# Chunks of 64 on quarters of the array, and other PSUM banks, in a linear-attention and mixture-of-experts layer

## The reference

```python
# attention: 8 heads of 32, q, k, v = layernorm(x) @ W.T
for chunk of 64 rows:
    inter  = q @ state                      # state: 32 x 32 per head
    scores = (q @ k.T) * tril
    intra  = scores @ v
    state  = state + k.T @ v
o     = inter + intra
denom = max(|sum(q * cumsum(k))|, 1)        # per row and head
o     = rmsnorm(o / denom, norm_w) @ Wo.T
x     = x + layernorm(o)
# experts: 8, all computed for every row, weighted by a router
h     = silu(y @ Wg[e]) * (y @ Wu[e])       # y = layernorm(x); 256 -> 256
out   = sum_e route[e] * (h @ Wd[e])
x     = x + layernorm(out)
```

## Time and profile before

| | us |
|---|---|
| three runs, median (lowest to highest) | 1700.5 (1697.83 to 1701.41) |
| the profiled execution | 1699.92 |
| its span, first to last instruction | 1698.2 |
| PE busy | 1621.4 (95%) |
| DVE busy | 1042.9 (61%) |
| ACT busy | 743.0 (44%) |
| POOL busy | 453.2 (27%) |

### The profile page before, as it was taken

How to read it: one execution, slowest core, us unless ns; L and a number is a source line. 1 busy time by engine, 2 the same in 40 slices (tenths; PEclk the granted TensorE clock), 3 DMA queues, 4 the chain that set the end, 5 groups by cost and what they waited for, 6 DMA issues and landing times. The chain is left out here.

```text
span 1698.2 us, 30395 instructions
## 1 busy us (share of the span) xinstructions
PE 1621.4 (95%) x10432; PEld 1424.6 (84%) x10432; DVE 1042.9 (61%) x2518; ACT 743.0 (44%) x1552; POOL 453.2 (27%) x750
## 2 busy tenths in 40 slices
PE   5599999999999999999999999999999999999987
PEld 4578888888888888888888888888888888888876
DVE  3555756657565665756666565666756666565655
ACT  5443544434344444444444344343534444354422
POOL 1321412324132231402323131232412223141230
PEclk9599999999999999999999999999999999999989
DMA  3200000000000000000000000000000000000000
GB/s 118 81 1 1 13 12 12 12 0 25 0 12 12 12 12 0 19 6 12 12 5 20 0 12 12 12 12 0 25 0 12 12 12 12 0 12 14 1 13 13
DMA packets 25339, 24.49 MB, mean 14 GB/s; under 512 B 2016, under 2 KB 25056, under 8 KB 25312
## 3 DMA queue, kind: packets, MB, share of 16 engines
q1 hardware_dynamic: 25312, 24.13, 4.5%
HBM read 15.74 MB, written 8.39 MB: 14 GB/s over the span
## 5 line engine op out<-in xcount | busy, mean ns | idle before, releaser
L843 DVE TENSOR_TENSOR late<-late,up_ps 128x512 f32<-128x512 f32 x256 | 174.8, 683 | 320.9 <-ACT late L648 319.1
L648 ACT ACTIVATE late<-gate_ps 128x512 f32<-128x512 f32 x256 | 152.1, 594 | 472.0 <-PE up_ps L387 448.1
L1040 POOL TENSOR_TENSOR rms_f<-rms_in,minus_half 128x8 f32<-128x8 f32 x64 | 112.1, 1752 | 698.0 <-DVE rms_in L805 698.0
L387 PE MATMUL down_ps<-w_hi,h_hi 128*128 128x256 f32 x1024 | 277.3, 293 | 8.4 <-DVE late L856 7.0
L387 PE MATMUL down_ps<-w_hi,h_lo 128*128 128x256 f32 x1024 | 263.2, 280 | 0.0
L761 DVE TENSOR_TENSOR h_lo<-late,h_hi 128x512 fp32r<-128x512 f32 x256 | 175.9, 687 | 116.2 <-ACT h_hi L566 114.0
L387 PE MATMUL gate_ps<-ft_hi,w_hi 128*128 128x512 f32 x512 | 211.7, 413 | 0.8 <-ACT ft_hi L566 0.8
L566 ACT ACTIVATE h_hi<-late 128x512 fp32r<-128x512 f32 x256 | 160.6, 627 | 117.8 <-DVE late L843 117.8
L387 PEld LDWEIGHTS down_ps<-w_hi,h_hi 128*128 128x128 f32 x1024 | 192.9, 188 | 16.6 <-DVE h_lo L761 9.0
L387 PE MATMUL gate_ps<-ft_hi,w_lo 128*128 128x512 f32 x512 | 203.7, 398 | 0.0
L387 PE MATMUL down_ps<-w_lo,h_hi 128*128 128x256 f32 x1024 | 203.6, 280 | 0.0
(11 more groups left out here) (144 smaller groups left out, 2956.1 us busy)
## 6 DMA issues: line engine op xcount, KB each, us to landing
xs<-in_x SPq DMA_DIRECT2D x32, 256.0 KB, 2.8
out_rows<-late SPq DMA_DIRECT2D x32, 256.0 KB, 2.2
late<-in_wg SPq DMA_DIRECT2D x8, 256.0 KB, 3.0
late<-in_wu SPq DMA_DIRECT2D x8, 256.0 KB, 2.7
late<-in_wd SPq DMA_DIRECT2D x8, 256.0 KB, 2.8
late<-in_wkv_t SPq DMA_DIRECT2D x1, 512.0 KB, 5.1
late<-in_wq_t SPq DMA_DIRECT2D x1, 256.0 KB, 3.3
late<-in_wo_t SPq DMA_DIRECT2D x1, 256.0 KB, 5.5
```

The source lines that it names most:

```text
L387: last = nc.tensor.matmul(dst, lhs, rhs, start=n == 0, stop=n == len(terms + low_terms) - 1)
L648: nc.scalar.activation(h_f[:, m, :], gate_ps[m][:, :], ACT.Silu).then_inc(silu_ready[0], 1)
L843: nc.vector.tensor_tensor(h_f[:, m, :], h_f[:, m, :], up_ps[m][:, :], ALU.mult).then_inc(h_ready[0], 1)
L1040: nc.gpsimd.tensor_tensor(rms_f[:, t % 2, :], rms_in[:, :], minus_half[:, :], ALU.pow)\
```

## The change

1. **Chunks of 64.** Each tile of 128 rows is two chunks, i = 0 and 1. The scores are 64 x 64 blocks, made in quarters of the array: 64 rows of contraction (r) and 64 weight columns (i), 16 matmuls a tile of 64 moving columns where there were 8 of 128. su becomes 8 matmuls of 64 x 64 weights with 66 moving columns where there were 2 of 128 x 128 with 132, and o becomes 4 state products of 128 x 64 weights and 132 moving columns and 16 products of prob and v in quarters, where there were 2 and 8.
2. **State.** DVE's su step makes two masked sums (528 values) and adds twice, since each chunk has a state of its own. o(t) now waits for su(t), so su stands ahead of o in `STEPS`, which is reordered throughout its first 19 places, as is the first block's list.
3. **kz.** Two copies with a per-partition factor (`odd_even`) instead of four copies of 32 partitions.
4. **PSUM.** One bank for gate, one for down, two for up, and four for attention as two pairs, where each step uses the first 256 columns of both banks of its pair. q and kv, of 512 columns, become two products of 256 columns each.
5. **Waits.** PE waits for silu of the gate before ahead of each gate, and for the reading of the down before ahead of each down. silu waits for gate alone (`gate_done`), hidden for up. add_down(0, 0) moves ahead of hidden(1, 1) on DVE. The last expert's written-out order goes; it is as every other.
6. **o_n, fin and prob** share an SBUF tensor, and DVE's places 1 to 3 in `first_expert` are now called.

```diff
 STEPS = [
     [("xt", 0), ("xt", 1)],
     [("kv", 0), ("q", 0)],
-    [("q", 1)],
-    [("kt", 0), ("kv", 1)],
-    [("s", 0, 0), ("s", 0, 1)],
-    [("kt", 1)],
-    [("o", 0), ("su", 0)],
-    [("s", 1, 0), ("s", 1, 1)],
-    [("kv", 2), ("keep_x1",), ("norm_stats", 0)],
-    [("kt", 2), ("o", 1), ("su", 1), ("norm_apply", 0)],
-    [("s", 2, 0), ("s", 2, 1)],
-    [("ot", 0), ("norm_stats", 1), ("kv", 3)],
-    [("kt", 3), ("o", 2), ("su", 2), ("norm_apply", 1)],
-    [("s", 3, 0), ("s", 3, 1)],
+    [("kv", 1), ("q", 1)],
+    [("kt", 0), ("su", 0)],
+    [("s", 0), ("kt", 1)],
+    [("su", 1)],
+    [("o", 0), ("s", 1)],
+    [("kv", 2), ("keep_x1",)],
+    [("kv", 3), ("norm_stats", 0)],
+    [("o", 1), ("kt", 2)],
+    [("su", 2), ("norm_apply", 0)],
+    [("s", 2), ("kt", 3), ("norm_stats", 1)],
+    [("ot", 0), ("su", 3)],
+    [("o", 2), ("s", 3), ("norm_apply", 1)],
     [("ot", 1), ("norm_stats", 2)],
-    [("o", 3), ("su", 3), ("norm_apply", 2), ("norm_stats", 3)],
-    [("wo", 0), ("ot", 2), ("norm_apply", 3)],
-    [("ln2_stats", 0)],
-    [("ln2_apply", 0), ("ot", 3)],
+    [("o", 3), ("norm_apply", 2)],
+    [("wo", 0), ("ot", 2), ("norm_stats", 3)],
+    [("norm_apply", 3), ("ln2_stats", 0)],
+    [("ot", 3), ("ln2_apply", 0)],
     [("ln2_add", 0), ("ln3_stats", 0)],
     [("wo", 1), ("ln3_apply", 0), ("ln2_stats", 1)],
...
-        gate_ps = [bank(f"gate_ps{m}") for m in range(MT)]
+        gate_ps = bank("gate_ps")
         up_ps = [bank(f"up_ps{m}") for m in range(MT)]
-        down_ps = [bank(f"down_ps{p}") for p in range(2)]
-        att_ps = [bank(f"att_ps{n}") for n in range(2)]
+        down_ps = bank("down_ps")
+        att_ps = ctx.enter_context(nc.psum_tensor("att_ps", [P, 4, 512], f32))
...
                 elif kind == "s":
-                    t, half = step[1:]
-                    if half == 0:
-                        return
+                    t = step[1]
                     reach(pe, q_ready, a, HG)
                     reach(pe, kz_ready, a, t + 1)
+                    pe.sem_inc(quarters_begun, 1)
+                    for n in range(2 * HG):
+                        g, j = divmod(n, 2)
+                        for i in range(2):
+                            for r in range(2):
+                                half = slice(64 * r, 64 * r + 64)
+                                tok = t * P + C * i
+                                last = nc.tensor.matmul(dst[C * i:C * i + C, r, C * n:C * n + C],
+                                                        kz[half, g, j, C * i:C * i + C], q_t[half, g, tok:tok + C],
+                                                        start=True, stop=True)
+                elif kind == "o":
+                    t = step[1]
+                    reach(pe, prob_ready, a, t + 1)
+                    reach(pe, v_ready, a, t + 1)
+                    reach(pe, state_ready, a, t + 1)
+                    for i in range(2):
+                        for g in range(HG):
+                            tok = t * P + C * i
+                            nc.tensor.matmul(dst[C * g:C * g + C, i, 0:HPG * VA], q_t[:, g, tok:tok + C],
+                                             state[:, t % B, t // B * 2 + i, :, g * PAIR:g * PAIR + PAIR],
+                                             start=True, stop=False)
+                    for j in range(HPG):
+                        for g in range(HG):
+                            for i in range(2):
+                                chunk = slice(C * i, C * i + C)
+                                last = nc.tensor.matmul(dst[C * g:C * g + C, i, j * VA:j * VA + VA],
+                                                        prob[chunk, j // 2, 2 * g + j % 2, :], v_sb[chunk, t, g * HPG + j, :],
+                                                        start=False, stop=j == HPG - 1)
+                elif kind == "su":
+                    t = step[1]
+                    reach(pe, v_ready, a, t + 1)
+                    pe.sem_inc(quarters_begun, 1)
...
             def up(e, m, f):
...
+                reach(pe, ft_hi_ready, f, 2)
+                reach(pe, silu_ready, f, 2 * e + m)
+                into(gate_ps, 0).then_inc(gate_done[0], 1)
+                reach(pe, h_ready, f, 2 * e + m - 1)
+                into(up_ps[m], 1).then_inc(up_done[0], 1)
 
             def down(e, p, f):
                 reach(pe, h_lo_ready, f, 2 * e + 2)
-                reach(pe, down_read, f, 2 * e + p - 1)
+                reach(pe, down_read, f, 2 * e + p)
...
             def rest(a, f):
 
-                for e in range(2, E - 1):
+                for e in range(2, E):
                     for m in range(MT):
                         up(e, m, f)
                         attention(4 * e - 4 + 2 * m, a)
                         down(e - 1, m, f)
                         attention(4 * e - 3 + 2 * m, a)
-
-                up(E - 1, 0, f)
-                up(E - 1, 1, f)
-                down(E - 2, 0, f)
-                for n in range(4 * E - 8, 4 * E - 4):
-                    attention(n, a)
-                down(E - 2, 1, f)
...
                 elif kind == "kt":
-                    for j in range(HPG):
-                        r = slice(j * D, j * D + D)
-                        last = copy(kz[r, :, j % 2, :], src[r, 0:HG * P].rearrange("p (g s) -> p g s", g=HG))
+                    for j in range(2):
+                        last = nc.scalar.activation(kz[:, :, j, :], src[:, :, 0:P], ACT.Copy, scale=odd_even[:, j:j + 1])
...
                 elif kind == "su":
                     t = step[1]
+                    b, n = t % B, t // B * 2
                     reach(dve, att_done, a, number_of(step, a) + 1)
...
+                    shape = [P, 2, 2, HG * PAIR]
+                    nc.vector.tensor_tensor(state_add[:, :, :, :],
+                                            att_half(step, a)[:, :, 0:HG * PAIR].unsqueeze(2).broadcast_to(shape),
+                                            pair_diag[:, :, :, :].broadcast_to(shape), ALU.mult).then_inc(su_read[0], 1)
                     reach(dve, su_read, a, t + 1)
...
+                    settle(nc.vector.tensor_tensor(state[:, b, n + 1, :, :], state[:, b, n, :, :], state_add[:, 0, :, :],
+                                                   ALU.add))
+                    nc.vector.tensor_tensor(state[:, b, (n + 2) % 4, :, :], state[:, b, n + 1, :, :], state_add[:, 1, :, :],
+                                            ALU.add).then_inc(state_ready[0], 1)
...
                 route_rank(f)
                 route_weights(f)
+                add_down(0, 0, f)
+                if a is not None:
+                    attention(1, a)
                 hidden(1, 1, f)
+                if a is not None:
+                    attention(2, a)
                 low_hidden(1, 1, f)
-                add_down(0, 0, f)
                 add_down(0, 1, f)
+                if a is not None:
+                    attention(3, a)
```

More of the change, by code:

```diff
@@ L31 @@
 VA = D + 1
-GV = HPG * VA
+C = 64
+PAIR = 2 * VA
 LN_EPS = 1e-5
@@ L291, in build_program @@
             READ_OUT["kt", t] = (kz_ready, t + 1)
-            for g in range(HG):
-                READ_OUT["s", t, g] = (prob_ready, HG * t + g + 1)
+            READ_OUT["s", t] = (prob_ready, t + 1)
             READ_OUT["o", t] = (o_copied, t + 1)
@@ L408, in att_step @@
                     reach(pe, xt_ready, a, KT)
-                    last = products(dst[:, :], [((wq_hi[:, k, g * P:g * P + P], wq_lo[:, k, g * P:g * P + P]),
-                                                 (xt_hi[:, k, :], xt_lo[:, k, :])) for k in range(KT)])
+                    for n in range(2):
+                        c = slice(256 * n, 256 * n + 256)
+                        last = products(dst[:, n, :], [((wq_hi[:, k, g * P:g * P + P], wq_lo[:, k, g * P:g * P + P]),
+                                                        (xt_hi[:, k, c], xt_lo[:, k, c])) for k in range(KT)])
                 elif kind == "kv":
@@ L413, in att_step @@
                     reach(pe, xt_ready, a, KT)
-                    last = products(dst[:, :], [((xt_hi[:, k, t], xt_lo[:, k, t]), (wkv_hi[:, k, :], wkv_lo[:, k, :]))
-                                                for k in range(KT)])
+                    for n in range(2):
+                        c = slice(256 * n, 256 * n + 256)
+                        last = products(dst[:, n, :], [((xt_hi[:, k, t], xt_lo[:, k, t]), (wkv_hi[:, k, c], wkv_lo[:, k, c]))
+                                                       for k in range(KT)])
                 elif kind == "kt":
@@ L436, in att_step @@
                 elif kind == "o":
                     t = step[1]
-                    reach(pe, prob_ready, a, HG * t + HG)
+                    reach(pe, prob_ready, a, t + 1)
                     reach(pe, v_ready, a, t + 1)
-                    reach(pe, state_ready, a, t - B + 1)
-                    for g in range(HG):
```

(22 more changed lines are left out.)

180 lines of the change are left out of this document (78 added, 102 removed).

## The result

| | before | after |
|---|---|---|
| median of the runs on one chip (lowest to highest), us | 1700.8 (1697.8 to 1701.4) | 1750.7 (1749.1 to 1752.6) |
| span of the profiled execution, us | 1698.2 | 1748.0 |
| mean granted clock, share of 2.4 GHz | 0.979 | 0.951 |
| matmul records in a middle pass of PE's loop | 652 | 880 |
| mean length of a middle pass, from tanh to tanh of the router, us | 101.28 | 105.85 |

The change made the kernel slower: ratio 1.0297, 95% interval 1.0280 to 1.0315. The prediction was 1660, faster; 1750.7 also lies outside its range of 1635 to 1733.

What follows compares the result with a forecast made beforehand. It took PE's instruction stream to bound each block. Array work -77, wait (a) +33, wait for v -22, wait (b) +24, tail +3.5, first block -2: -40.5 on 1699.9 gives 1660 us, range 1635 to 1733.

Steps and rivals of the forecast that it cites:

- The step that failed: A middle block, 101.29 us, is PE's instruction stream end to end; DVE and ACT matter only where PE waits for them.
- (a): down(0,1) waits until DVE has read the down before it with the router's weights: 2.2 us (1.8 to 2.6), +33 us.
- (b): End of a block: down(5,1) waits 1.3 us, ft(1) 0.2, and 0.1 for norm order; 1.6 in all, +24 us.
- The array work: Attention's matmuls in quarters save 8.0 us a block, changes of array division add 2.9: net 5.1 less, 77 us in all.
- Rivals 1, 2 and 3: Column halves not side by side (1728 or 1755, chance 0.17); every start needs 0.03 (1732, 0.10); nothing overlaps (1890, 0.04).
- rival 4: Division changes cost twice 0.39 on six added visits, or (a) and (b) reach 6.3 a block: 1698, chance 0.09.
- the 1713: Total in us if each matmul takes about 60 cycles, 0.025 us, however small; a case of every start needing a fixed time.
- The wait for v: Tile 0's score matmuls stand 1.5 us for a copy of v, 15 times; forecast to go, -22 us.
- The first block: PE is busy 39 of 60 us there; it gains some from ACT and DVE: -2 us (0 to -5).
- The tail: Last block: work moved behind the down's router wait, less the faster chain, +3; the last down waits for the read, +0.5.
- q and kv in halves: Splitting q and kv into twice as many 256-column products costs nothing (bounds 0.4 us a block either way).
- ACT and DVE: ACT 49 us less from kz's copies, DVE 10 us more from state_add and a second add, all beside PE.

Runs made afterwards that it cites:

- e2: The changed kernel with PE's loop over the blocks written out: 1677.6 us, ratio 0.9891 to before.
- e4: The kernel before with PE's loop over the blocks written out: 1696.6 us, ratio 1.0003 to before.
- e5: The kernel before with the q and kv products issued as two halves of 256 columns: 1698.9 us, ratio 1.0005.
- e10: e9 with up(2,0) placed between attention's third and fourth piece of the first expert: 1673.4 us, ratio 0.9866 to before.
- e8: e7 with norm_stats(3) back beside o(3) and ln3_apply(0) moved one place later: 1664.5 us, ratio 0.9801 to before.
- e1: The kernel before with all 512-column gate, up, q and kv products made as two of 256, 880 records a pass: 1716.3 us, ratio 1.0122.
- e7: The changed kernel with up(2,0) moved to the end of PE's loop pass and down(0,1) put behind it: 1680.7 us, ratio 0.9900 to before.
- e3: The changed kernel without the ranking of the experts, so without the wait (a): 1702.7 us, ratio 1.0036 to before.
- e9: e8 with PE's loop written out: 1663.6 us, ratio 0.9811 to before.
- e11: The kernel before with q, kv and all gate products as column halves, 784 records a pass: 1703.7 us, ratio 1.0029.

## Why the prediction was wrong

**The step that failed** is the first one, "So a block is PE's instruction stream, end to end", carried into the sum without a term for how that stream reaches PE: the 228 records by which the body of the loop grows are priced as time on the array alone. It holds in the earlier trace rows, where the body of the loop fits, and no longer with 880 records a pass. Two costs came that stand in none of the sum's terms, in 13 middle passes: the stop at the head of the loop, 3.6 us on average, and the low clock around it, 2.6. The low clock came in the last block too, which is outside the loop and has only the data waits (101.73 us, in e2 99.06). From e2 to after the span grows by 72 us (1676.0 to 1748.0), and that is the main part of the 90 us by which the forecast was short. "PE's idle time per block is far from 4 us" was named as what would make it wrong, and so it was: (a), the stop and (b) come to some 8.

**The array work: right.** Forecast 5.1 us less a block. Scores alone 0.77 (0.85 forecast), o 1.39 (1.4), su 0.59 (0.61), o with scores behind it 1.89 (1.88), which is 747.72 to 749.61 in the rows above, counted from the slot behind the last up to the first slot of the down. All visits of a block: 4 x (1.29 + 2.69) = 15.9 before, 4 x 0.59 + 2 x (0.77 + 1.39 + 1.89) = 10.5 after, 5.5 less. Rivals 1, 2 and 3 are out: 32 quarter records start in 0.48, not in 0.9 or more. So is rival 4: su with its changes of division costs what was forecast, and (a) and (b) come to 4.5 us, not 6.3.

On the price of a small matmul: records start 0.015 apart, less than 0.025. The Trainium skill, "TensorEngine Tiling (Array Packing)", Instruction Overhead, has about 60 cycles for each matmul, 0.025 at 2.4 GHz. Counted by record the trace contradicts it, and so the 1713 that rests on it is out. Counted by the program's fp32 matmuls, two records each, it is 0.03, and the runs leave open whether the page means that.

**(a): right.** Forecast 1.8 to 2.6 with 2.2 taken; measured 1.95 to 2.0 by the starts. The wait for v went, as forecast. **(b): right in kind, short in size.** down(5, 1) waits 1.57 (1.3), ft(1) at most 0.1 (0.2), but ot(3) waits 0.61 for the norm whose statistics were put one place later, and ft(0) 0.37 for its layer norm. These two were overlooked: 1 us a block, 15 in all. With them the sum would have given about 1675, and e2, which has everything but the stop at the head, measured 1677.6. That these agree so well is in part luck: the middle passes fell short of the sum and the first block went beyond it. A middle pass of e2 is on average 0.8 us shorter than before's, where the terms with the two waits give 1.8. The low clock takes 0.9, and the array (0.4) and (a) (0.2) give some back. Another 0.8 is in no term: a pass of e2 at the full clock is 99.6, 1.7 shorter than before's, while the measured terms (5.5 and 1.5 less, 2.0 and 2.5 more) would make it 2.5. Of that the transposes of k and of o account for 0.5 (1.3 before, 1.7 after) and the halves for 0.1.

**The first block: right in sign, far too small.** It was put at -2 (0 to -5). The router's first tanh comes at 81.7 us in after and in e2, at 94.8 in before and at 91.3 in e4: 10 to 13 us earlier. Up to there the clock is at 0.71 in before and at 0.75 in after, and PE is busy 58.5 and 43.1 us, so the attention's smaller work counts there too, at the slower clock; the sum had it for 15 blocks only. The tail came as forecast (from the last tanh to the end 82.9 in before, 86.5 in after; +3.5 forecast).

**q and kv in halves: right**, at the body's present length. e5 has 0.1 us a pass for it. But the 36 records belong to the 228 that overfill the loop, so "costs nothing" was wrong as a statement on the kernel.

**ACT and DVE: right in that they stay beside PE.** Their sizes were off, at no cost: ACT -34 us (-49 forecast), DVE -1 (+10 forecast). Silu of the one gate bank made no wait in after; e10 shows how near it was.

## What to carry to other kernels

Count the instructions of a loop's body before and after a change, on the engine that bounds the kernel, and look at the instruction queue in the table of DMA queues: no packet in a middle pass before, nine after, is where the diagnosis begins. Packets alone do not prove a cost, for the written-out loops have them too; a stop at the head of the body, once for each branch back, does. And look at what lies behind such a stop before you price its removal: in e8 a data wait took its place. A body that is too long need not be made shorter. Write the loop out, or put its branch behind the longest work that can be queued. And price a stop of the bounding engine with its clock: in after two stops of 2.0 and 3.6 us cost another 2.6 in slow matmuls, so removing one of them returned more than its own length.

## What the runs showed of the hardware

- PE's loop bodies of 652 to 784 matmul records are not fetched again in the middle passes (16 to 19 packets in the whole run; one run of 736 fetched its body a second time, once, 27 packets); bodies of 880 are, nine packets of 16 KB a pass, in e1 as in after.
- The first matmul behind the branch came 2.6 to 3.2 us after the beginning of an instruction packet, in every stop of after, e1, e7 and e8. How much of that PE stood depended on what was queued ahead of it: 3.3 to 4.0 us behind 0.7 us of short matmuls, 1.6 to 1.8 behind a row of 256-column ones (0.9 to 1.4 in e7 and e8), none to 1.6 behind 2.8 us of 512-column ones.
- The granted clock. With stops of 2.0 and 3.3 to 4.0 us a few us apart it was at the 1.2 GHz level around them in every middle pass of after, for 2.6 us of lost time on average. After the long one alone (e3) 1.4 us were lost in every pass; with (a) and (b) alone, 2.0 and 1.6 (e2), nothing in 6 passes of 13 and 1.3 to 2.8 in the others, in three of them behind (b). In e7, e8, e9 and e11, where the longest stop was 1.6 or less, no middle pass lost anything. What decides between the passes of e2 isn't shown.
- Quarters of the array work four at a time for fp32, loads and multiplications both: 0.45 to 0.48 us from the first start to the last of 32 records of 64x64 with 33 or 64 columns. Going into the divided array and out of it costs 0.3 to 0.4 a visit, as it did with halves.
